# Spreading the last half group of keys of an attention batch over two pairs of heads

## What is computed

```
q = split_heads(query @ Wq + bq);  k = split_heads(bank @ Wk + bk);  v = split_heads(bank @ Wv + bv)
scores = jnp.einsum('bhqd,bhkd->bhqk', q, k) / scale
attn = jax.nn.softmax(scores, axis=-1)
out = jnp.einsum('bhqk,bhkd->bhqd', attn, v) @ Wo + bo
x = _layernorm(x + out)
```

## Time and profile before

| | us |
|---|---|
| median of 3 runs | 2209.33 (2198.43 to 2209.99) |
| the profiled execution | 2207.1, of which span 2205.3 |
| one attention batch (b = 6, first layer) | 64.46 |
| PE busy in the span | 2080.2 (94%) |
| DVE, ACT, POOL busy | 1020.0, 951.6, 785.3 (46%, 43%, 36%) |
| mean granted TensorE clock | 0.986 |

### The profile page before, as it was taken

How to read it: one execution, slowest core, us unless ns; L and a number is a source line. 1 busy time by engine, 2 the same in 40 slices (tenths; PEclk the granted TensorE clock), 3 DMA queues, 4 the chain that set the end, 5 groups by cost and what they waited for, 6 DMA issues and landing times.

```text
span 2205.3 us, 36789 instructions
## 1 busy us (share of the span) xinstructions
PE 2080.2 (94%) x12700; PEld 1921.8 (87%) x12700; DVE 1020.0 (46%) x1685; ACT 951.6 (43%) x1663; POOL 785.3 (36%) x635
## 2 busy tenths in 40 slices
PE   4899999999889999899999999899999999999997
PEld 4788888888778778788888888899999999999987
DVE  8566666666673576466566666556100003000032
ACT  2356565556662444455565655422222223111141
POOL 0434333234456345323443332322232232222244
PEclk9999999999999899999999999999999999999999
DMA  5465555446321212754655554212111112111123
GB/s 174 132 166 154 151 137 156 135 136 162 109 67 29 80 30 86 217 141 131 163 153 155 137 154 121 69 58 66 58 57 64 60 57 64 60 57 62 61 76 97
DMA packets 140378, 233.86 MB, mean 106 GB/s; under 512 B 49240, under 2 KB 93528, under 8 KB 140184
## 3 DMA queue, kind: packets, MB, share of 16 engines
q1 hardware_dynamic: 140312, 232.99, 36.9%
HBM read 174.12 MB, written 55.53 MB: 104 GB/s over the span
## 4 chain that ended last, share of the span: by engine, by line
PE 77%; DVE 8%; ACT 5%; issue 3%; POOL 3%; DMA 3%; SPq 1%; DVEq 0%; POOLq 0%; ACTq 0%
PE psS L345 14%; PE psS L347 14%; PE psS L346 14%; PE psO L1925 5%; PE psJ L345 4%; PE psJ L346 3%; PE psJ L347 3%; PE psS L1884 3%; PE psT L1911 2%; PE psT L345 2%; PE psT L347 2%; PE psT L346 2%; PE psS L1911 2%; PE psO L346 1%; PE psO L345 1%
## 5 line engine op out<-in xcount | busy, mean ns | idle before, releaser
L797 POOL TENSOR_TENSOR fw_lo<-raw,fw_hi 128x1024 fp32r<-128x1024 f32 x96 | 236.3, 2461 | 543.2 <-ACT fw_hi L1108 543.2
L345 PE MATMUL psS<-hid_hi,fw_hi 128*128 128x400 f32 x1152 | 396.8, 344 | 3.5 <-DVE hid_lo L1807 2.9
L347 PE MATMUL psS<-hid_hi,fw_lo 128*128 128x400 f32 x1152 | 397.8, 345 | 0.0
L346 PE MATMUL psS<-hid_lo,fw_hi 128*128 128x400 f32 x1152 | 397.4, 345 | 0.0
L589 POOL TENSOR_TENSOR pT<-p,pT 128x600 fp32r<-128x600 f32 x128 | 188.8, 1475 | 531.6 <-ACT pT L896 530.2
L1335 DVE TENSOR_REDUCE psS<-psS 100x1 f32<-100x722 f32 x256 | 234.7, 917 | 153.7 <-PE psS L1884 153.3
L1807 DVE TENSOR_TENSOR hid_lo<-h_act,hid_hi 128x800 fp32r<-128x800 f32 x32 | 38.5, 1272 | 530.3 <-ACT hid_hi L1231 530.3
L345 PEld LDWEIGHTS psS<-hid_hi,fw_hi 128*128 128x128 f32 x1152 | 216.2, 188 | 7.4 <-DVE hid_lo L1807 5.1
L347 PEld LDWEIGHTS psS<-hid_hi,fw_lo 128*128 128x128 f32 x1152 | 217.5, 189 | 0.0
L346 PEld LDWEIGHTS psS<-hid_lo,fw_hi 128*128 128x128 f32 x1152 | 216.1, 188 | 0.0
L345 PE MATMUL psJ<-cT_hi,wk_hi 128*128 128x362 f32 (+1 forms) x512 | 181.4, 354 | 36.3 <-DVE cT_lo L1329 15.6
(11 more groups left out here) (347 smaller groups left out, 4448.7 us busy)
## 6 DMA issues: line engine op xcount, KB each, us to landing
kS<-k_parts SPq DMA_DIRECT2D x384, 180.5 KB
raw<-ffn_dram SPq DMA_DIRECT2D x96, 512.0 KB, 3.6
k_parts<-kst SPq DMA_DIRECT2D x64, 362.0 KB, 3.4
k_parts<-kst SPq DMA_DIRECT2D x64, 360.0 KB, 3.0
ctx_raw<-ctxT_dram SPq DMA_DIRECT2D x32, 361.0 KB, 4.0
qS<-q_parts SPq DMA_DIRECT2D x192, 50.0 KB, 2.6
q_parts<-qst SPq DMA_DIRECT2D x16, 400.0 KB, 2.5
ctx_late<-ctxT_dram SPq DMA_DIRECT2D x14, 362.0 KB, 5.0
```

The costliest lines, as they stand in the source:

```text
L345: nc.tensor.matmul(out, st[0], mv_[0], start=first, stop=False)
L346: nc.tensor.matmul(out, st[0], mv_[1], start=False, stop=False)
L347: return nc.tensor.matmul(out, st[1], mv_[0], start=False, stop=last)
L797: nc.gpsimd.tensor_tensor(fw.lo[:, e, :], raw[:, e, :], fw.hi[:, e, :], ALU.subtract)\
```

## The change

`KEYS_AT` gets pair 3, so that half group (3, 1) is issued over pairs 2 and 3: chunk 0 and chunk 1 in the two slots of pair 2, chunk 2 and chunk 3 in the two slots of pair 3 (`KEY_CHUNKS`). Its high and low parts are made in pair 3 (`KEYS_DONE_AT`). In pair 4, ACT and POOL split only chunks 0 and 1 of the second half of the context ahead of the odd head's exponentials and low part, and chunks 2 and 3 behind them. The weights of the feed-forward block move from pairs 2 and 3 to pairs 3 and 4.

```
-KEYS_AT = {0: (2, 1), 1: (3, 0), 2: (3, 1)}
+KEYS_AT = {0: (2, 1), 1: (3, 0), 2: (3, 1), 3: (3, 1)}
+KEYS_DONE_AT = {0: (2, 1), 1: (3, 0), 3: (3, 1)}
+KEY_CHUNKS = {2: ((0,), (1,)), 3: ((2,), (3,))}
-FFN0_AT = {2: 0, 3: 1, 5: 2, 6: 3}
+FFN0_AT = {3: 0, 4: 1, 5: 2, 6: 3}
...
# POOL, batch
                         if t == 4 and not last:
-                            for c in range(C):
+                            for c in (0, 1):
                                 half_lo(b + (NB - 1) * L, c, 1)
                         odd_probs_lo(L, b, t)
+                        if t == 4 and not last:
+                            for c in (2, 3):
+                                half_lo(b + (NB - 1) * L, c, 1)
...
-                        if L == 0 and last and t - 1 in (2, 3):
+                        if L == 0 and last and t - 1 in (3, 4):
                             split_ffn0(FFN0_AT[t - 1])
...
# ACT, batch
                         even_probs(b, t)
                         if t == 4 and not last:
-                            for c in range(C):
+                            for c in (0, 1):
                                 half_hi(L, b + 1, c, 1)
-                        if t in KEYS_AT:
-                            keys_hi(L, b, *KEYS_AT[t])
+                        if t in KEYS_DONE_AT:
+                            keys_hi(L, b, *KEYS_DONE_AT[t])
...
                             max_rows(b, t + 1)
                             if not last:
                                 half_hi(L, b + 1, 3, 0)
+                        if t == 4 and not last:
+                            for c in (2, 3):
+                                half_hi(L, b + 1, c, 1)
...
-                            if t == 2:
+                            if t == 3:
                                 act.wait_ge(A.v_mm, NKC * NB)
                                 act.wait_ge(A.k_mm, 2 * C * NB)
...
# DVE, batch
-                        if t in KEYS_AT:
-                            keys_lo(L, b, *KEYS_AT[t])
+                        if t in KEYS_DONE_AT:
+                            keys_lo(L, b, *KEYS_DONE_AT[t])
...
# PE, batch
-                            keys(L, ahead[1], *ahead[0], cs=(0, 1))
+                            keys(L, ahead[1], *ahead[0], cs=KEY_CHUNKS.get(t, ((0, 1), (2, 3)))[0])
...
-                            keys(L, ahead[1], *ahead[0], cs=(2, 3))
+                            keys(L, ahead[1], *ahead[0], cs=KEY_CHUNKS.get(t, ((0, 1), (2, 3)))[1])
```

## The result

The changed kernel takes 2260.6 us (median of 4 runs, 2256.3 to 2265.3), the kernel before 2209.7. The ratio is 1.0237 (95% interval 1.0204 to 1.0270): slower by some 51 us. I had said slower by 37, 2246 us, with 2261 as the upper end. The profiled execution took 2264.0 us with a span of 2262.1 and a mean granted clock of 0.974 (before 2207.1, 2205.3 and 0.986).

The account below looks back on a forecast made before the run. PE was taken as the bound, busy 62.48 of 64.46 us a batch. Steady batches 24.6, batches 0 3.3, last batches 6.0 and block u2 2.8 made 36.7 us, giving 2246 us; 8 in 10 range 2227 to 2261.

Parts of the forecast that it names:

- The bound and the direction: PE sets the pace with at most 2.0 us of gaps a batch; pair 3, full on ACT, ends 0.2 us later.
- Pair 5: PE waits for POOL's late context chunks and head 12's keys; the delays overlap, costing 2.1 us a batch.
- Batches 0 and last: Later keys delay head 12: +1.3 and +2.0 us in batches 0, +3.0 us in each layer's last batch.
- the weights: First layer's last batch: block u2 loads later and ACT waits for it ahead of pair 7's exponentials, +2.8 us.
- The sum of order: All delays from the changed order over both attentions, together 36.7 us.
- rival (d): Keys in take 5.8 us, or PE's clock falls at its new stands: 2258, 2261 or 2273 us; chance 0.13.
- The stand of 1.3 us that I forecast for head 12: At the top of pair 5, PE stands 1.3 us for the transfer of keys in.
- A clock under 1.00 in the attention: Listed sign in the profile after that the forecast was wrong: PE's clock under 1.00 in the attention.
- (a): PE's gaps in pair 3 are filled and nothing new waits: 20 us faster, 2189 us; chance 0.06.
- (b): Nothing measurable: pair 2's gain of 0.7 us kept, stall behind half absorbed later, about 2209 us; chance 0.05.
- (c): Chain in pair 3 holds, POOL costs 1 us or less a batch: 2225 us, 2228 at most; chance 0.1.

Follow-up runs that it names:

- e1: Changed kernel with all four chunks of the second context half ahead of the odd head again in pair 4, on ACT and POOL: 2253.9 us, ratio 1.0216.
- e6: Kernel before, on SP alone: last keys out wait for DVE's low part of pair 3, late context load goes ahead of them: 2258.7 us, ratio 1.0240.
- e2: Kernel before with only chunks 2 and 3 of the second context half behind the odd head in pair 4: 2259.8 us, ratio 1.0229.
- e5: Changed kernel with dummy matmuls at each place where PE was seen to stand in the attentions: 2249.9 us, ratio 1.0194.
- e3: Kernel before with only the feed-forward weights a pair later in the first layer's last batch: 2213.0 us, ratio 1.0033.
- e9: e2 with eight dummy matmuls ahead of head 12's scores in each batch that has a next one: 2239.2 us, ratio 1.0148.
- e10: Kernel before with dummy matmuls where PE stands outside the steady batches: 2216.2 us, ratio 1.0029.
- e8: Changed kernel with chunks 2 and 3 of half group (3, 1) both in the first slot of pair 3: 2271.3 us, ratio 1.0277.
- e4: Changed kernel with six dummy matmuls ahead of head 12's scores in each batch that has a next one: 2259.1 us, ratio 1.0235.

## Why the prediction was right and wrong

**The bound and the direction: right.** PE had 2.0 us of gaps a batch, pair 3 was full on ACT, and what went into it pushed the maxima back by 0.34 us (forecast 0.2).

**Pair 5: right.** The last chunks came 2.24 us late (forecast 2.1) and head 12 at 515.98 (515.8). SP went on 528.48 - 525.09 = 3.4 us after keys out (forecast 3.6), and head 12's scores began 532.99 - 528.48 = 4.5 us after keys in (4.3 and the wake-up). The estimate by the Trainium skill (DMA: Bandwidth & Descriptors, "Anatomy of one DMA — SWDGE (gpsimd) path", a fit for GpSimd's queue) was 3.3 us for these three transfers; on SP's queue the trace shows 4.5 from the first issue to PE's start, and the measurement decides. e1 and e6 show the transfer's delay without POOL's, 1.7 and 1.4 us a batch, e2 shows POOL's alone, 2.0. The sum is 3.4 to 3.7, together they cost 2.3: they overlap, as the sum had it.

**Batches 0 and last.** Batches 0 cost 0.5 and 1.5 us in e5 (forecast 1.3 and 2.0), the last ones 4.9 and 2.7 (5.8 and 3.0). e3 has 2.7 us for the weights (2.8), but with two waits for raw blocks where e5 has one of 2.1 us; how the 4.9 divides isn't shown. In the changed kernel's own trace ACT waits for no raw block in that batch, against the forecast: 14.3 us of it ran at half clock, and ACT waited for PE instead (11.0 us in all for the maxima, 6.2 in e5).

**The sum of order: right, the last tenths by luck.** 36.7 forecast, 36.8 in e5. Two parts were off and cancel: the steady batches cost 2.3 us in the first layer and 2.2 in the second, 27 in all (24.6), the others 9.6 (12.1).

**The step that failed is the clock.** The sum had no term for it; I set it aside as rival (d), because "the clock is 1.00 over the whole batch with its gaps". Those gaps were 0.54, 0.72 and 0.26 us. The new ones were 0.97 and 1.0 to 1.5, and that row says nothing of them. Elsewhere the trace of the kernel before did. Between the attentions PE waited 0.89 us for DVE from 814.6, and 1.3 us after that wait the half clock began:

```profile
813.40:816.80 3.40, 2.51 (x19) 1.82 (x18) 3.40 (x7) 1.44 (x3) 0.81 (x2) 1.00 0.07 15
816.80:823.60 6.80, 6.80 (x26) 5.20 (x24) 4.45 (x9) 1.07 (x2) 4.89 (x4) 0.50 0.24 53
```

The stand of 1.3 us that I forecast for head 12 is longer than that. The order itself was priced; that PE then works some of the time at half clock was not, and the runs put it at 15.6 us in the attentions: 52.4 in the changed kernel, 36.8 in e5, whose steady batches never leave the full clock. e5 takes 10.7 us back in the medians with the same order, e9 takes 20.6 from e2. "A clock under 1.00 in the attention" stood in my own list of signs of being wrong, and it came. My bound for it, 15 us on the sum, was the right size: 2246 + 15 = 2261, where it stands. That is luck: it was half of what the clock lacks over the whole span, not worked out from the new stands. Its chance should have been the larger one. Between e5's 2249.9 and the 2244 of order alone stand 6 us. Its six runs go from 2242.7 us at a mean clock of 0.987 to 2255.5 at 0.981, with the traced one at 2244.8. The kernel before spreads in the same way: 2202 us at 0.988 to 2218 at 0.981 in the seventeen runs beside e9 and e10. Where in a run the clock is lost then isn't shown, since one run of each kernel was traced.

Rivals (a), (b) and (c) are out by the 66.8 us batch at full clock. Transfers slower than forecast, the other half of (d), are out by the 4.5 us. What stays open is when exactly the clock falls: in e2, batches with the same waits ran with 0, 3.4, 6.8 or 10.2 us of it.

## What to carry to other kernels

Filling an idle slot helps only if what leaves the slot has no deadline. Here the work moved into PE's gap was the first link of a chain through two engines and two transfers. Keys out went 4.2 us later and head 12 began 1.65 us later, so the slack of that chain was 2.5 us; POOL's was 1.6. Price a wait on TensorE twice: its length, and what PE then loses at half clock; dummy matmuls in the same place separate the two. A batch that is 0.4 us shorter at full clock, but with one stand of 1.6 to 2.0 us in it, came out some 0.3 us longer on average (e8). And compare the stretch that was changed as well as the whole: code that nobody touched varied by 15 us between traces.

## What the runs showed of the hardware

- The granted clock of TensorE fell from 2.4 to 1.2 GHz (1.00 to 0.50) in steady batches, each time behind a stand of 0.89 to 2.04 us. It did not fall in the steady batches of the kernel before, whose longest stand was 0.72 to 0.79. It fell in one of e4's twelve (stands of 0.9 to 1.0), in seven of the changed kernel's (1.0 to 1.5), ten of e2's (1.7) and eleven of e8's (1.6 to 2.0). The stretches lasted 3.4 to 10.2 us in a steady batch.
- What it cost: the changed kernel's attentions against e5's, 15.6 us for 45.9 us more at half clock; e2's against e9's, 29.6 us for 65.9.
- Keeping PE busy with dummies in the stands removed all of them from the steady batches (e5, e9), at 0 to 0.2 us a batch against the same batch at full clock without them.
- Dummies outside of them removed low stretches there and others came, one of 13.7 us in e10. In it PE was busy for 12.96 of 13.70 us, and it began while PE stood 2.38 us for a transfer.
